# A two-layer Mamba block: carry preparation on four 64x64 array tiles, and a new rule for handing out PSUM banks

## The reference, cut to what matters

```
delta = softplus(dbc[..., :16] @ dtw + dtb);  Bm, Cm = the next 16 and the last 16 columns of dbc
dA = exp(delta[..., None] * -exp(a_log))
mi = delta[..., None] * Bm[:, :, None, :] * xb[..., None]
v = 0.6 * v + mi_t          # first recurrence, over time
h = dA_t * h + v            # second recurrence, over time
y_t = einsum('ben,bn->be', h, C_t)
y = (y + dp * xb) * silu(z);  out = y @ out_w
```

## Time and profile before

| | |
|---|---|
| median of 3 runs | 1577.21 us |
| profiled execution | 1579.04 us, of which its span 1577.5 us |
| PE busy in the span | 1427.5 us (90%) |
| DVE, POOL, ACT busy | 1081.6, 923.0, 897.0 us |
| the 8 sequences | first scan at 77.35 us, last T at about 1003 us |

### The profile page before, as it was taken

One profiled execution on the slowest core, in us unless ns is written; L12 is line 12 of the kernel. 1 busy time (PEld: TensorE's weight loads), 2 busy tenths in 40 slices (PEclk: granted clock), 3 DMA queues, 4 the chain that ended last, 5 costly groups with the idle time before them and its releaser, 6 DMA issues.

```text
span 1577.5 us, 44648 instructions
## 1 busy us (share of the span) xinstructions
PE 1427.5 (90%) x19348; PEld 999.3 (63%) x19348; DVE 1081.6 (69%) x1447; ACT 897.0 (57%) x1287; POOL 923.0 (59%) x802
## 2 busy tenths in 40 slices
PE   4869999999999999999999987878989887999997
PEld 2446676776776776777777775533434343489996
DVE  3298898698698798798797886677666771422223
ACT  2757667667667667667666655216555655434440
POOL 1269878979979979969969976630303000035541
PEclk8889999999999999999999998969999998999999
DMA  4011221222122212212221334470424100612225
GB/s 145 35 52 61 81 82 57 83 82 96 70 83 82 75 63 83 82 66 72 82 83 69 118 134 119 88 147 1 76 45 81 27 1 6 269 41 71 67 68 177
DMA packets 41489, 127.13 MB, mean 81 GB/s; under 512 B 8784, under 2 KB 21584, under 8 KB 32848
## 3 DMA queue, kind: packets, MB, share of 16 engines
q1 hardware_dynamic: 34736, 108.28, 21.3%
q0 software_dynamic: 6048, 14.95, 3.6%
q10 hardware_dynamic: 512, 1.05, 0.4%
HBM read 97.90 MB, written 9.57 MB: 68 GB/s over the span
## 4 chain that ended last, share of the span: by engine, by line
PE 60%; DVE 15%; POOL 9%; issue 9%; ACT 4%; DMA 3%; DVEq 0%; SPq 0%; ACTq 0%; POOLq 0%
PE psum L589 9%; PE psum L568 8%; POOL hst L953 5%; DVE hst L748 4%; PE psum L1264 4%; PE psum L1676 4%; PE psum L1688 3%; PE psum L522 3%; PE psum L559 3%; PE psum L491 3%; PE psum L533 3%; PE psum L1246 2%; PE psum L527 2%; DMA overlay<-x_hat,origin 2%; PE psum L1618 2%
## 5 line engine op out<-in xcount | busy, mean ns | idle before, releaser
L953 POOL TENSOR_TENSOR hst<-hst,cb 128x512 f32<-128x512 f32 x399 | 517.1, 1316 | 137.1 <-DVE hst L748 107.5
L748 DVE TENSOR_TENSOR_SCAN hst<-dA,psum 128x512 f32<-128x512 f32 x316 | 372.5, 1206 | 131.0 <-PE psum L589 130.7
L568 PE MATMUL psum<-ident,hst 128*128 128x128 f32 x1596 | 242.2, 283 | 19.4 <-POOL hst L953 11.4
L568 PEld LDWEIGHTS psum<-ident,hst 128*128 128x128 f32 x1596 | 176.9, 142 | 81.2 <-issue 42.8
L889 ACT ACTIVATE dA<-delta,alog 128x512 f32<-128x512 f32 x256 | 177.7, 719 | 57.2 <-DVE hst L748 29.9
L889 ACT ACTIVATE dA<-xres,alog 128x512 f32<-128x512 f32 x256 | 176.9, 719 | 39.3 <-DVE hst L748 23.2
L1385 DVE TENSOR_REDUCE nmax<-psum 128x2 f32<-128x1024 f32 x128 | 154.6, 1220 | 56.5 <-PE psum L1230 56.2
L1314 ACT ACTIVATE pT<-psum 128x1024 f32<-128x1024 f32 x128 | 128.0, 1024 | 103.1 <-PE psum L1250 79.4
L953 POOL TENSOR_TENSOR w_early<-w_early,cb 128x512 f32<-128x512 f32 x113 | 145.3, 1299 | 26.5 <-DVE w_early L748 22.9
L589 PE MATMUL psum<-filt,c_early 64*64 64x86 f32 (+1 forms) x6144 | 143.9, 238 | 13.3 <-DVE hst L748 5.5
L589 PE MATMUL psum<-filt,uT 64*64 64x86 f32 (+1 forms) x6144 | 145.2, 239 | 9.0 <-DVE w_early L748 2.6
(11 more groups left out here) (244 smaller groups left out, 2333.7 us busy)
## 6 DMA issues: line engine op xcount, KB each, us to landing
cb<-c_rows SPq DMA_DIRECT2D x64, 1024.0 KB, 4.7
qk_first<-w_early SPq DMA_DIRECT2D x64, 64.0 KB, 2.4
qk<-part SPq DMA_DIRECT2D x64, 64.0 KB, 2.6
w_up<-up_dram SPq DMA_DIRECT2D x8, 512.0 KB, 7.3
w_down<-down_dram SPq DMA_DIRECT2D x8, 512.0 KB, 13.8
w_up<-y_choice SPq DMA_DIRECT2D x8, 512.0 KB, 7.4
qk<-part POOLq DMA_DIRECT2D x48, 64.0 KB, 5.3
qk_first<-part SPq DMA_DIRECT2D x40, 64.0 KB, 2.4
```

Source lines behind the costliest of these rows:

```text
L568: m = pe.matmul(psum[:, Y0 + et % EP, t * P:(t + 1) * P], hst(i)[:, t * P:(t + 1) * P], ident[:], start=n == 0 and t == 0, stop=n == NSTAT ...
L748: dve.tensor_tensor_scan(hst(i), a, v, 0.0, ALU.mult, ALU.add).then_inc(scan_done, 1)
L953: pool.tensor_tensor(h, h, cb[:, q % 2, state_of(i)[1] % GN, :], ALU.mult).then_inc(g_done, 1)
```

## The change

Five parts:

1. `u` is done in 64x64 tiles: 16 matmuls a chunk with 64 columns each, on all four tiles, and two chunks in one piece. Upper and lower rows of the array write different banks.
2. `mid` uses rows 0 to 63 alone, in two column tiles of 256 columns each; `bend` has two groups of 64 columns. `c` is 4 matmuls on the four tiles, 256 columns each, with the two halves of time in two banks (`c` and `ch`), in every sequence. ACT now copies 16 x 256 pieces: 2 for `mid`, 4 for a carry.
3. These pieces (`TILED`) stand right behind the product pair, ahead of both T's.
4. Banks are given out by `banks_for`: a product pair gets the neighbouring two that have been idle longest, any other piece the idlest one. No scan is split any more.
5. `y` waits for its own tile of delta, not for all four.

```diff
+TILED = ("u", "mid", "c", "ch")
+def banks_for(rows, banks):
+    at, left_by, count, last, oldest = {}, {}, {}, {}, list(range(banks))
+    todo = [(name, who) for name, who in rows]
+    second = None
+    for name, who in todo:
+        count[who] = count.get(who, 0) + 1
+        if second is not None:
+            q, second = second, None
+        elif who == "scan":
+            q = min((b for b in oldest if b + 1 in oldest), key=lambda b: max(oldest.index(b), oldest.index(b + 1)))
+            second = q + 1
+        else:
+            q = oldest[0]
+        oldest.remove(q)
+        oldest.append(q)
+        at[name], left_by[name] = q, last.get(q)
+        last[q] = (who, count[who])
+    return at, left_by
...
                 for c in range(NCH):
-                    put(43 + c, "pe", "u", c)
-                    put(44 + c, "act", "u", c)
+                    put(44 + c // 2 * 2, "pe", "u", c)
+                    put(45 + c // 2 * 2, "act", "u", c)
...
                 for c in range(NCH - 1):
-                    put(52 + 2 * c, "pe", "c", c)
-                    put(53 + 2 * c, "act", "c", c)
+                    for part in ("c", "ch"):
+                        put(52 + 2 * c, "pe", part, c)
+                        put(53 + 2 * c, "act", part, c)
...
                 elif what == "u":
-                    bk = pe_open(k, "u", j)
+                    if j % 2:
+                        return
+                    sides = [pe_open(k, "u", j + half) for half in range(2)]
...
-                    for e in range(ET):
-                        for half in range(2):
-                            t0, r0 = half * HS + CHUNKS[j][0], half * KT
-                            i = pe.matmul(bk[r0:r0 + KT, e * P:(e + 1) * P], uw[:, e, t0:t0 + KT], ident[:], start=True, stop=True, tile_position=(0, r0))
-                elif what in ("c", "ch"):
-                    bk = pe_open(k, what, j)
-                    cols = carry_cols(k, what)
-                    pe.wait_ge(bank_act, emptied_by("act", k, what, j - 1) if j else emptied_by("act", k, "mid", 0))
-                    i = pe.matmul(bk[:, cols], bend[:, j, :], uT[par][:, j, cols], start=True, stop=True)
+                    for c in range(2):
+                        for e in range(ET):
+                            for half in range(2):
+                                for rows0 in range(0, P, KT):
+                                    t0, c0 = half * HS + CHUNKS[j + c][0], c * HS + e * KT
+                                    i = pe.matmul(sides[rows0 // KT][half * KT:(half + 1) * KT, c0:c0 + KT], uw[rows0:rows0 + KT, e, t0:t0 + KT],
+                                                  ident[rows0:rows0 + KT, rows0:rows0 + KT], start=True, stop=True, tile_position=(rows0, half * KT))
...
                     for c in range(NCH):
-                        i = pe.matmul(bk, bend[:, c, :], uT[par][:, c, :], start=c == 0, stop=c == NCH - 1)
+                        for e0 in range(2):
+                            i = pe.matmul(bk[e0 * MT:(e0 + 1) * MT, e0 * HS:(e0 + 1) * HS], bend[0:KT, c, MID:MID + MT], uT[par][0:KT, c, e0 * HS:(e0 + 1) * HS],
+                                          start=c == 0, stop=c == NCH - 1, tile_position=(0, e0 * MT))
+                elif what == "c":
+                    sides = [pe_open(k, part, j) for part in ("c", "ch")]
+                    pe.wait_ge(bank_act, emptied_by("act", k, "ch", j - 1) if j else emptied_by("act", k, "mid", 0))
+                    for e0 in range(2):
+                        for half in range(2):
+                            r0 = half * KT
+                            i = pe.matmul(sides[half][e0 * MT:(e0 + 1) * MT, e0 * HS:(e0 + 1) * HS], bend[r0:r0 + KT, j, 0:MT],
+                                          uT[par][r0:r0 + KT, j, e0 * HS:(e0 + 1) * HS], start=True, stop=True, tile_position=(r0, e0 * MT))
...
+                        for x in pair_steps(i):
+                            if x[1] in TILED:
+                                pe_side(*x)
                     if i >= LAG:
                         pe_add_state(i - LAG)
                     for x in steps["pe"].get((k, i % TILES), []):
-                        pe_side(*x)
+                        if x[1] not in TILED:
+                            pe_side(*x)
...
-                    act.wait_ge(delta_done, ET * min(k + 2, NI))
+                    act.wait_ge(delta_done, ET * (k + 1) + j + 1 if k + 1 < NI else ET * NI)
...
+            def act_carry(dst, bk):
+                for e0 in range(2):
+                    cols = slice(e0 * HS, (e0 + 1) * HS)
+                    i = act.copy(dst[0:NSTATE, cols], bk[e0 * MT:e0 * MT + NSTATE, cols])
+                i.then_inc(bank_act, 1)
```

More of the change, by code:

```diff
@@ L190, in build @@
             toep = sb(mc, "toep", [P, QC])
-            ends = sb(mc, "ends", [P, NCH, 3])
+            ends = sb(mc, "ends", [P, NCH, 2])
             keep = sb(mc, "keep", [P, 1])
@@ L468, in emptied_by @@
             def emptied_by(who, *name):
-                assert emptied[place[name]][0] == who
-                return emptied[place[name]][1]
+                assert emptied[name][0] == who
+                return emptied[name][1]
             def filled(*name):
@@ L614, in pe_mamba @@
                             m.then_inc(bank_full, 1)
-            def carry_cols(k, what):
-                if k:
-                    return slice(0, DI)
-                return slice(0, DI // 2) if what == "c" else slice(DI // 2, DI)
             def tiles_of(k, part):
@@ L725, in build @@
             VINC = 2 * P // MT
-            split_before = list(itertools.accumulate(place["v", i - i % 2] % NRING == NRING - 1 for i in range(NI * TILES)))
-            def wraps(i):
-                return split_before[i]
             def dve_mamba():
@@ L744, in dve_mamba @@
                     a, n = dA[:, i % NDA, :], i % 2
-                    b0 = place["v", i - n] % NRING
-                    if b0 < NRING - 1:
-                        v = psum[:, b0:b0 + 2, :].rearrange("p b (t n) -> p n (b t)", n=2)[:, n, :]
-                        dve.tensor_tensor_scan(hst(i), a, v, 0.0, ALU.mult, ALU.add).then_inc(scan_done, 1)
-                    else:
-                        v0, v1 = (bank("v", i - n + half).rearrange("p (t n) -> p n t", n=2)[:, n, :] for half in range(2))
-                        h = hst(i)
-                        dve.tensor_tensor_scan(h[:, 0:HS], a[:, 0:HS], v0, 0.0, ALU.mult, ALU.add).then_inc(half_done, 1)
-                        dve.wait_ge(half_done, wraps(i))
-                        dve.tensor_tensor_scan(h[:, HS:S], a[:, HS:S], v1, h[:, HS - 1:HS], ALU.mult, ALU.add).then_inc(scan_done, 1)
+                    b0 = place["v", i - n]
+                    v = psum[:, b0:b0 + 2, :].rearrange("p b (t n) -> p n (b t)", n=2)[:, n, :]
+                    dve.tensor_tensor_scan(hst(i), a, v, 0.0, ALU.mult, ALU.add).then_inc(scan_done, 1)
                     for x in steps["dve"].get((i // TILES, i % TILES), []):
```

57 lines of the change are left out of this document (32 added, 25 removed).

## The result

The changed kernel takes 1556.74 us (median of 4 runs, 1554.73 to 1566.52), the kernel before, beside it, 1577.22 (4 runs, 1576.11 to 1578.87). The ratio is 0.988 with a 95% interval of 0.985 to 0.992. The forecast was 1525, the range 1509 to 1553: the sign was right, the size wrong, and the time lies outside the range. The profiled execution's span is 1555.7 us, 21.8 shorter than before.

The account below looks back on a forecast made before the run. The prediction took POOL and PE to bound each sequence in turn. 47.3 us in the loop, 4.6 from scans and 0.8 ahead of it, 52.7 off 1579.04, gave 1526.3, in the runs' terms 1525; range 1509 to 1553.

Parts of the forecast that it names:

- What bounds the kernel: In each sequence POOL bounds up to the last uw, then PE through `u`, `mid`, carries and the next projections.
- What PE saves: In one preparation: `u` 3.9 us, `mid` 2.6, carries 2.15, sum 8.6; with product 44 moved, 9.6 us earlier.
- What of it counts: T of the next state 0 moves up at most 2.65 + 4.12 us; 6.75 for 7 preparations, 47.3 us.
- ACT, banks, order, `y`: In the loop: ACT's copies take 1.6 us off PE's spare saving; banks and order cost 0; `y` gains 0.
- Scans: On DVE, unsplit scans save 0.51 us a pair; 9 of 50 pairs count, 4.6 us, the other 41 zero.
- Ahead of the loop: Before the loop `u` gains 1.8 us, `mid` 2.6, the carries lose 3.6; net 0.8 us gained.
- rival 1: Only POOL's 2.65 us gap goes, as ACT or DVE feed POOL no earlier; 24 us gained, 1553; chance 0.15.
- Rival 2: Tiled `u` is bound per record at 28 ns, a block 1.8 us; 10.5 us less gained, 1535; chance 0.12.
- Rival 3: POOL catches up and all 9.6 us of PE's saving a sequence count; 72 us gained, 1505; chance 0.08.
- Rival 5: The tiles on PE don't overlap; 7 x 8 us more, some 1630; chance 0.01.
- Rival 4: `u`, `mid` and carries ahead of T wait for banks or `uT` and block PE's queue; slower, 1613; chance 0.05.
- What would show it: Right: no POOL gap at state 52, sequences of about 108 us; wrong: above 111 us or a gap that stays.

Follow-up runs that it names:

- before_banks: The kernel before the change, with only the banks given out by idle time, so no scan is split: 1566.2 us.
- before_mid: The kernel before the change, with only the middle state's product in two column tiles and its copy in two pieces: 1561.5 us.
- bo_later: The changed kernel with the output products `bo` two states later in PE's order, nothing else: 1540.3 us.
- untied: The changed kernel with `u`, `mid` and the carries back at their own states, behind half of T: 1558.2 us.
- gate_bo: The changed kernel with POOL's last two gates of a sequence two states earlier and `bo` two states later: 1536.5 us.

## Why the prediction was wrong, step by step

**What bounds the kernel.** Half right. PE and POOL in turn, handed over at the first `u`: the rows after agree. The second hand-over was missed. It says "Behind it PE and DVE are full for 17.6 us, nothing there is shortened, and the shift arrives whole". PE was full, but not by its own pace alone: the `bo` in the midst of that stretch started 0.10 us after a gate on POOL.

**What PE saves.** Right in kind, a little high: 7.5 us a sequence measured (111.81 - 104.32) for 8.6. `u` 3.7 us and not 2.7, the carries 0.54 to 0.60 and not 0.43, `mid` right. To this come `u`'s stops of "issue", 0.9 us a sequence.

**What of it counts: the step that failed.** It took T of the next state 0 as the only thing for which PE waits on POOL, found 4.12 us of slack there, and added them to the gap: 6.75 us. T did move up: where it had trailed POOL by 4.1 us, it now trails by 0.15 us in two sequences, as forecast, and by 2.2 to 3.9 in the others. But that wasn't what held the sequence, since `bo` had a slack of zero. Only the 2.65 came, and the split scans' 0.9 that before_banks measured (115.4 - 2.65 - 0.9 = 111.85, and 111.8 it is); in every second sequence the clock took 1.5 back. Six sequences gained 18.6 us instead of 44 (18.2 by the mark at state 33). before_mid, which saves PE only 2.3 us, got 13.8 of these; bo_later, which saves no more than the change, got 38.1 by the mark at state 33. The cause is shown from both sides.

**ACT, banks, order, `y`.** That they cost nothing came out right, but for a reason other than that named: untied shows 2 us a sequence without effect, thanks to the wait at `bo`. The change to `y` wasn't run by itself. Before, PE waited 6.7 us for it in six sequences, after not at all; the sum above leaves nothing over for it.

**Scans.** 4.6 us forecast, 10.7 measured by before_banks. The 41 split pairs that I set to zero were not all free: by its sequences alone it is 0.9 us each, some 6 for the seven. By what way they hold PE wasn't taken apart.

**Ahead of the loop.** The first sequence starts 0.8 us earlier (first scan at 76.59 us, before 77.35), 0.8 was forecast, but by luck: the first carry starts 5.4 us earlier (61.22, before 66.66), where `u` and `mid` were to give 4.4, and the carries lose 4.6 us, not 3.6. The first two take 2.4 us, near the 2.3 forecast, the last three 2.8 to 2.9, at the clock's lower level. The first row is a window, as above, the others PE's timeline; PE waits 1.72 us ahead of each of the last four carries:

```profile
68.00:72.00 4.00, 1.43 (x12) 0.67 (x16) 0.00 (x0) 2.13 (x6) 0.00 (x0) 0.50 0.00 0
```

```profile
65.99 1.13 PE L569 MATMUL psum<-c_early,overlay 64*64 64x256 f32 x8 [1.72 <-ACT c_early L802]
68.84 1.13 PE L569 MATMUL psum<-c_early,overlay 64*64 64x256 f32 x8 [1.72 <-ACT c_early L802]
```

**Rivals.** The time is nearest to rival 1's 1553, and its amount, the gap alone, is what came. Its reason (ACT or DVE feed POOL no earlier) was wrong: POOL was fed without a break, and PE stood. Rival 2 had a block of `u` at 1.8 us; it takes 1.10 to 1.31 without its stops. The Trainium skill ("TensorE: Matmul & The Clock Gate", section "Wait — 56ns, not 53.3ns?") gives a floor of about 25 ns from start to start. The trace disagrees: 64 records in 1.10 us are 17 ns each, and 20 with the slower blocks. Rival 3 didn't come either: with both edits, gate_bo, a sequence is 106.9 to 108.9 us, where all 9.6 us would have made it 105.9. Rival 5 is refuted by `mid`. Rival 4's mechanism, a piece ahead of T that blocks the queue, does exist at `bo`, which it left out.

**The range.** It ended at rival 1's 1553, "only the gap goes". With the gate seen, that would have been the middle, with the clock as a loss on top (some 1.5 us in three sequences).

**What would show it.** Of its signs of being wrong the first came, a sequence above 111 us. That PE would stand ahead of `bo` stood in neither of its lists.

## What to carry over

When an engine gets faster, list every wait on its queue in the stretch where its partner falls behind, not only the one that the partner's gap points to; a `[0.20 <-issue]` ahead of a long instruction, whose releaser ended 0.10 us earlier, is a wait at zero slack. Then move that instruction, since the saved time stands right in front of it: one row of the order was worth 16 us here, and 2 without the change. And spare time is local: 2 us in hand at one place say nothing of another place in the same queue.
